# Soft combine: subtracting the maxima of the last logit tiles on VectorE instead of in TensorE's accumulation

## The reference

```python
def _L1_ffn_ref(x, phi_w, phi_b, expert_w, expert_b):      # x: tokens x 128
    logits = x @ phi_w.T + phi_b                 # tokens x 2048, seen as (n = 64 experts, p = 32 slots)
    D = softmax(logits over p)                   # dispatch weights
    C = softmax(logits over n)                   # combine weights
    X_tilde = layernorm(clip(D.T @ x)); X_tilde = tanh(X_tilde)
    Y_tilde = X_tilde[n] @ expert_w[n] + expert_b[n]       # 2048 slots x 128
    return C @ Y_tilde
```

## Time and profile before

| | |
|---|---|
| median of 3 executions | 2280.3 us (2280.26, 2280.30, 2286.44) |
| profiled execution | 2283.84 us, its span 2281.8 us |
| PE busy | 1911.1 us (84%) |
| DVE busy | 1573.7 us (69%) |
| ACT busy | 1187.5 us (52%) |
| POOL busy | 1204.3 us (53%) |
| logits, f32 products (L1889) | 512 records, 261.8 us |
| logits, bf16 products (L1890) | 256 records, 96.8 us |
| combine (L1916) | 512 records, 226.7 us |

### The profile page before, as it was taken

One profiled execution on the slowest core, in us unless ns is written; L12 is line 12 of the kernel. 1 busy time (PEld: TensorE's weight loads), 2 busy tenths in 40 slices (PEclk: granted clock), 3 DMA queues, 4 the chain that ended last, 5 costly groups with the idle time before them and its releaser, 6 DMA issues.

```text
span 2281.8 us, 24245 instructions
## 1 busy us (share of the span) xinstructions
PE 1911.1 (84%) x6152; PEld 923.1 (40%) x6152; DVE 1573.7 (69%) x2040; ACT 1187.5 (52%) x2832; POOL 1204.3 (53%) x779
## 2 busy tenths in 40 slices
PE   4099676888888725978999899997987999899998
PEld 3077522333333513764333344443333333344443
DVE  7033487999999831338999665764895999855544
ACT  2322286555555341217999643342446999753332
POOL 4645104999999574535999400000983999800000
PEclk9999896999999957989999999998988999999999
DMA  8122472444545122333000000001633000000000
GB/s 263 57 88 89 109 129 110 174 176 169 180 168 177 54 68 67 102 119 93 0 0 0 1 1 1 0 0 51 180 111 90 3 0 0 0 1 10 5 9 14
DMA packets 108478, 163.50 MB, mean 72 GB/s; under 512 B 11144, under 2 KB 74051, under 8 KB 108273
## 3 DMA queue, kind: packets, MB, share of 16 engines
q1 hardware_dynamic: 100210, 146.29, 21.4%
q0 software_dynamic: 8192, 16.30, 2.1%
HBM read 124.97 MB, written 38.14 MB: 71 GB/s over the span
## 4 chain that ended last, share of the span: by engine, by line
PE 49%; DVE 21%; issue 13%; POOL 11%; ACT 3%; DMA 2%; DVEq 0%; POOLq 0%; SPq 0%; ACTq 0%
PE ps L1916 10%; PE ps L1889 10%; PE ps L1645 5%; PE ps L1655 5%; PE ps L1845 4%; DVE arena L1396 3%; PE ps L1836 3%; DVE arena L1402 3%; DVE arena L1394 3%; POOL slot_inputs L504 3%; PE ps L1771 3%; PE ps L1890 2%; DVE arena L1341 2%; POOL arena L558 2%; POOL arena L594 1%
## 5 line engine op out<-in xcount | busy, mean ns | idle before, releaser
L1845 PE MATMUL ps<-arena 128*128 128x512 f32 x512 | 250.9, 613 | 14.3 <-POOL arena L558 14.2
L1889 PE MATMUL ps<-XT,c_phiT 128*128 (+1 forms) x512 | 261.8, 593 | 0.0
L1836 PE MATMUL ps<-c_phiT,arena 128*128 128x512 f32 x512 | 245.9, 604 | 9.7 <-DVE arena L1396 7.0
L566 POOL TENSOR_TENSOR arena<-arena 128x864 f32<-128x864 f32 x128 | 210.1, 1642 | 78.5 <-DVE arena L1394 75.8
L558 POOL TENSOR_TENSOR arena<-arena 128x1024 f32<-128x1024 f32 x128 | 244.6, 1912 | 0.0
L532 POOL TENSOR_TENSOR arena<-XT,arena 128x1024 f32<-128x1024 f32 x86 | 169.7, 1993 | 134.6 <-DMA arena<-input_gates 134.6
L1916 PE MATMUL ps<-arena 128*128 128x512 f32 x512 | 226.7, 601 | 11.1 <-DVE arena L1460 11.1
L594 POOL TENSOR_TENSOR arena<-arena 128x1024 f32<-128x1024 f32 x32 | 63.6, 2000 | 309.9 <-DMA arena<-value_rows 309.9
L1460 DVE TENSOR_TENSOR arena<-arena 128x4096 f32<-128x4096 f32 x32 | 140.2, 4422 | 121.0 <-ACT arena L899 121.0
L892 ACT ACTIVATE arena<-ps 128x512 f32<-128x512 f32 x256 | 152.0, 597 | 111.4 <-PE ps L1890 111.3
L514 POOL DMA_INDIRECT token_outputs<-arena x128 | 124.3, 971 | 148.3 <-DVE arena L1236 114.7
(11 more groups left out here) (229 smaller groups left out, 3597.3 us busy)
## 6 DMA issues: line engine op xcount, KB each, us to landing
arena<-input_gates SPq DMA_DIRECT2D x128, 512.0 KB, 3.8
arena<-value_rows SPq DMA_DIRECT2D x32, 512.0 KB, 4.8
arena<-slot_inputs SPq DMA_DIRECT2D x32, 258.0 KB, 2.8
arena<-in_L_ffn_w SPq DMA_DIRECT2D x32, 256.0 KB, 4.0
arena<-token_outputs SPq DMA_DIRECT2D x16, 512.0 KB, 7.4
slot_inputs<-arena SPq DMA_DIRECT2D x1, 4128.0 KB, 13.4
slot_inputs<-zero SPq DMA_DIRECT2D x1, 4128.0 KB, 33.3
token_outputs<-arena SPq DMA_DIRECT2D x1, 4096.0 KB, 17.5
```

Of the source, the lines that this page charges most:

```text
L566: pool.tensor_tensor(Ed[:, r, PSLOT * NA:].rearrange("p (n q) -> p n q", q=PSLOT), Lc[:, r, PSLOT * NA:].rearrange("p (n q) -> p n q", q=P ...
L1836: ins = pe.matmul(pbank(2 * h + c), xts[:, r // 2, :], phiT[:, at:at + CHUNK], start=True, stop=True)
L1845: ins = pe.matmul(pbank(4 + 2 * h + c), xns[:, r // 2, :], Dd[:, r, CHUNK * c:CHUNK * (c + 1)], start=start, stop=stop, skip_group_check=True)
L1889: pe.matmul(pbank(t % 4), phiT[:, P * t:P * (t + 1)], xt(b, c), start=True, stop=False)
```

## The change

In the six chunks of the loop, the last tiles of a chunk lose their bf16 product. `BY_PE = (11, 9)` is the number of tiles that keep it: in stage 0 tiles 11 to 15 (5 of them) go without, in stage 1 tiles 9 to 15 (7 of them). In place of these products:

- TensorE does the bf16 product once more, alone, into bank 4, ahead of tile 4. It waits for the logarithm of the chunk before (`lnz`), which was the last to read bank 4.
- ScalarE copies bank 4 into a new 128 x 512 tile `mS` in SBUF, ahead of the exponential of tile 6, after the wait for tile 6.
- VectorE adds `mS` to each of the last tiles, from PSUM into `Ec[c]` (`less_m`). In its order this stands at the start of a chunk, ahead of `ln_apply` and the tree.
- ScalarE's exponential of these tiles waits for the addition and runs in place on `Ec[c]`.

Some semaphores are merged: `Z` becomes `bank4`, `Rz` becomes `token_rows`, `g_diff` and `gates` in the experts become one. The experts' instructions stay as they were.

```diff
+BY_PE = (11, 9)
...
+        mS = cut([CHUNK])
...
                         if t == 0 and not first:
                             hold(act, sem("yT_ps"), v - 1)
-                        act.activation(Ec[c][:, t, :], pbank(t % 4), ACT.Exp)\
-                            .then_inc(sem("Ec"), 1)
+                        if not first and t == 6:
+                            hold(act, sem("bank4"), sums_count(s, v) - 1)
+                            act.activation(mS, pbank(4), ACT.Copy).then_inc(sem("token_rows"), 1)
+                        logit = pbank(t % 4)
+                        if not first and t >= BY_PE[s]:
+                            hold(act, sem("less_m"), less_m_count(s, v, t))
+                            logit = Ec[c][:, t, :]
+                        act.activation(Ec[c][:, t, :], logit, ACT.Exp).then_inc(sem("Ec"), 1)
...
+                def less_m(v, c):
+                    dve.wait_ge(sem("token_rows"), sums_count(s, v) - 1)
+                    dve.wait_ge(sem("yT_ps"), v - 1)
+                    for t in range(BY_PE[s], ST):
+                        dve.wait_ge(sem("LT"), ST * v + t + 1)
+                        dve.tensor_tensor(Ec[c][:, t, :], pbank(t % 4), mS, ALU.add).then_inc(sem("less_m"), 1)
...
                 with dve.Fori(1, CHUNKS // 2) as i:
+                    less_m(base + 2 * i, 0)
                     if s == 0:
                         ln_apply(4, 2 * i - 2, 0)
                     normalise(base + 2 * i, 0)
                     residual(base + 2 * i - 1, i - 1, 1)
+                    less_m(base + 2 * i + 1, 1)
...
-                        pe.matmul(pbank(t % 4), phiT[:, P * t:P * (t + 1)], xt(b, c), start=True, stop=False)
-                        pe.matmul(pbank(t % 4), row128[:, :],
-                                  mCT[:, ds(b * TIME + CHUNK * c, CHUNK)], start=False, stop=True).then_inc(sem("LT"), 1)
+                        m = mCT[:, ds(b * TIME + CHUNK * c, CHUNK)]
+                        if loop and t == 4:
+                            pe.wait_ge(sem("lnz"), v)
+                            pe.matmul(pbank(4), row128[:, :], m, start=True, stop=True).then_inc(sem("bank4"), 1)
+                        without_m = loop and t >= BY_PE[s]
+                        ins = pe.matmul(pbank(t % 4), phiT[:, P * t:P * (t + 1)], xt(b, c), start=True, stop=without_m)
+                        if not without_m:
+                            ins = pe.matmul(pbank(t % 4), row128[:, :], m, start=False, stop=True)
+                        ins.then_inc(sem("LT"), 1)
```

More of the change, by code:

```diff
@@ L296, in over, with sums_count, less_m_count @@
             return t.unsqueeze(2).to_broadcast([t.shape[0], t.shape[1], n])
+        def sums_count(s, v):
+            return v - CHUNKS * s + (2 * CHUNKS - 2) * s + 1 if isinstance(v, int) else 2 * (v - s)
+        def less_m_count(s, v, t):
+            return (ST - BY_PE[s]) * (v - CHUNKS * s - 2) + t - BY_PE[s] + 1 + s * (ST - BY_PE[0]) * (CHUNKS - 2)
         def below(i, n):
@@ L659, in experts @@
             def experts(m, k):
-                hold(act, sem("g_diff"), m + 1)
+                hold(act, sem("gates"), 2 * m + 1)
                 act.activation(g1[5], g1[4], ACT.Exp).then_inc(sem("g_exp"), 1)
@@ L665, in experts @@
                     chain(act.activation(A_neg[:, :, :], A_neg[:, :, :], ACT.Copy, scale=-1.0))
-                hold(act, sem("gates"), m + 1)
+                hold(act, sem("gates"), 2 * m + 2)
                 for q in range(K):
@@ L891, in exp_T @@
                             hold(act, sem("yT_ps"), v - 1)
-                        act.activation(Ec[c][:, t, :], pbank(t % 4), ACT.Exp)\
-                            .then_inc(sem("Ec"), 1)
+                        if not first and t == 6:
[6 more added lines that the diff above has]
+                        act.activation(Ec[c][:, t, :], logit, ACT.Exp).then_inc(sem("Ec"), 1)
                 def finish(v):
-                    hold(act, sem("Z"), v + 1)
+                    hold(act, sem("bank4"), sums_count(s, v))
                     act.activation(lnz, pbank(4), ACT.Ln).then_inc(sem("lnz"), 1)
                     hold(act, sem("lnz"), v + 1)
-                    act.activation(Rz, lnz, ACT.Exp, scale=-1.0).then_inc(sem("Rz"), 1)
+                    act.activation(Rz, lnz, ACT.Exp, scale=-1.0).then_inc(sem("token_rows"), 1)
                 def copy_y(v):
@@ L1201, in experts @@
                 ok = g64[1].rearrange("p (a b) -> p a b", b=TILES)
-                dve.tensor_tensor(d21, g1[1], g1[0], ALU.subtract).then_inc(sem("g_diff"), 1)
+                dve.tensor_tensor(d21, g1[1], g1[0], ALU.subtract).then_inc(sem("gates"), 1)
                 chain(dve.tensor_scalar(ok, place, CAP + 0.5, None, ALU.is_lt))
@@ L1456, in normalise @@
                         dve.tensor_tensor(dst, lo, hi, ALU.add).then_inc(sem("tree"), 1)
-                    dve.wait_ge(sem("Rz"), v + 1)
+                    dve.wait_ge(sem("token_rows"), sums_count(s, v))
                     for g in range(2):
@@ L1881, in soft, with logits_T @@
                 base = CHUNKS * s
-                def logits_T(v, b, c, early, beside=None):
+                def logits_T(v, b, c, early, beside=None, loop=False):
                     for t in range(ST):
@@ L1907, in total @@
                     pe.wait_ge(sem("tree"), 5 * (v + 1))
-                    pe.matmul(pbank(4), same_p[:, :], t1, start=True, stop=True).then_inc(sem("Z"), 1)
+                    pe.matmul(pbank(4), same_p[:, :], t1, start=True, stop=True).then_inc(sem("bank4"), 1)
                 def combine(v, c, early):
@@ L1938, in soft @@
                         v = base + 2 * i + c
-                        logits_T(v, i, c, False)
+                        logits_T(v, i, c, False, loop=True)
                         combine(v - 1, 1 - c, False)
```

## The result

| | before | changed |
|---|---|---|
| median, 6 executions each | 2285.14 us (2280.26 to 2287.33) | 2270.24 us (2269.16 to 2272.29) |
| profiled execution, its span | 2283.84, 2281.8 us | 2269.76, 2267.8 us |
| PE, DVE, ACT busy | 1911.1, 1573.7, 1187.5 us | 1901.0, 1618.9, 1192.8 us |

The ratio of the times is 0.994, 95% interval 0.993 to 0.9951: the changed kernel is 0.6% faster. The medians of six lie 14.9 us apart. Three further executions of the kernel before, taken beside the changed one, were at 2284.83 to 2287.33 us, above two of the three that the prediction started from.

What follows compares the result with a forecast made beforehand. TensorE alone was taken to bound the loops: net 60 products x 0.215 = 12.9 us, less 0.2 of stalls, so 2280.3 - 12.7 = 2267.6 us. The range was 2264.5 to 2272.5 us, the forecast's own 2266.5 to 2270.

Steps and rivals of the forecast that it cites:

- What bounds the kernel: Combine loops of both stages: TensorE alone sets the time, so a removed bf16 product is worth its full 0.215 us.
- The sum: Both stages' loops: 12.9 us from a net 60 products, less 0.2 us of small stalls, gives 12.7 us.
- the narrower range: Whole kernel's time with full gain but for small stalls: 2266.5 to 2270 us, chance 0.74.
- (a): Stage 0, tile 15: additions begin late, at 13.55 us into a chunk, leaving tile 15 a slack of 0.1 us.
- The exponential from SBUF: ScalarE, last tiles: reading SBUF instead of PSUM takes 0.63 instead of 0.60 us; the skill page estimates 0.04 more.
- The addition: VectorE, last tiles: each of 72 additions of 128 x 512 from PSUM takes 0.68 us.
- The slower case: VectorE's additions in both stages become the bound; above 1.46 us each the kernel is slower than before; chance 0.03.
- my formula: Waits by addition length L: stage 0's tile 15 L - 0.80 us, stage 1's 3L - 2.9 above L = 0.97.
- (b): Stage 1, tile 13: additions start when tile 9 is ready at 11.0 us, slack 0.5 us, and none falls behind.
- (c): End of a chunk: the tree ends later but before `total` needs it, slack 3.2 us in stage 0, 3.8 in stage 1.
- Rival 3: Outside the loops, between the stages: TensorE's clock drops move, changing the time by a few us; upward gain's chance 0.07.
- A reading: Profile slices of the combine: VectorE (DVE) was read at 5 to 9 in slices 23 to 27.

## Why the prediction was right

- **What bounds the kernel.** Right. Every product taken from TensorE's stream in the loops came back whole, at 0.215 us, in every trace.
- **The sum.** 12.7 us were forecast for the two loops, 12.5 measured: 4.80 of stage 0's 5.17 and 7.71 of stage 1's 7.74. The time itself fits less well, and that 2270.24 us lies in the range is in part luck. The predicted median, 2267.6 us, started from 2280.3, but the median of six executions of the kernel before is 2285.14, 4.8 higher; and the difference is 14.9 us and not 12.7, since stretches outside the loops gave 2.4 us. The two errors go against each other. The measured time is just above the narrower range of 2266.5 to 2270. The ratio, 0.994, agrees with the forecast's own 0.9944.
- **(a), the edge at tile 15.** The place was right, and two terms were mis-sized against each other. The exponential of tile 11 ended 15.09 us after the chunk's start in an odd chunk (15.15 forecast), because VectorE's end and ScalarE's start are 0.09 us apart and not 0.28, while the first addition started at 13.68 and not 13.55. There is no stall in odd chunks, though the weight load of tile 15 is 0.1 us late, so the slack is used up. In even ones VectorE's loop starts a round in just this gap, the addition starts at 14.08 and the exponential ends at 15.50: 0.18 us of stall, in chunks 4 and 6. I had 0.2 us for the sum of these, and 0.36 came.
- **The exponential from SBUF.** 627 against 597 ns, 0.03 us, as L899 had shown. The Trainium skill's 0.04 ("VectorE: DVE Perf Modes", section "The TRN2 errata — SBUF-src ops pay a fixed extra latency per instruction") has the sign and nearly the size.
- **The addition.** 690 ns against 0.68. The slower case would have needed 1.46 us by my formula. With each addition done twice, 1.20 us from pair to pair, the loops lost 5.0 of their 12.5 us, where the prediction had put 6.6 for an addition of 1.20. So the formula overstates the losses, by the 0.10 us now known between the engines among others; the 1.46 itself was not tried.
- **(b) and (c).** Right to 0.4 us: in stage 1 the additions wait for their tiles. The tree of stage 0 ends 26.95 us into the chunk (27.3 forecast) and the total comes at 30.49 (30.5). In stage 1 it is 25.5 (25.8) and 29.63 (29.6).
- **Rival 3**, a shift outside, was real, and it came on top of the forecast instead of in its place: -3.1 us between the stages, +0.6 ahead of stage 0 and +1.0 at the end, 1.5 us in all. The prediction had named a move of more than 2 us between the stages as a sign against its forecast; it came, and the loops still did what was forecast. Of the 3.1, 2.6 are of the kind that the rival names, a shift that moves TensorE's clock drops; 1.4 are not, but come from VectorE's loop in stage 1's dispatch, and 0.9 are lost again around it, most of them by the clock. At the end the granted clock over the last combine is 0.86 instead of 0.91, and the changed kernel's second trace has the same (28.11 us against 27.27 in the kernel before's). Between the stages and at the end the length repeats from trace to trace of a kernel. Ahead of stage 0 that isn't shown: there the 0.6 us are small against the 5 us by which kernels on one chip differ.
- **A reading.** VectorE's slices in stage 0's combine stand at 5 to 7, not 5 to 9. Nothing rests on it.

## What to carry to other kernels

Where one engine's stream has no gap, a piece of work moved off it is worth its distance in that stream; what it costs on the other engines is decided by when they are free, when their input is ready and when the result is needed back, counted from the start of a round, not by their busy share. When the helper is late, look first at what stands ahead of it in its own order: here 2.7 us of statistics moved behind three additions turned a loop that lost 6 us against the kernel before into one that gained 7.8. A few tenths of slack belong where the helper's own loop starts a round. And gains of one or two us are judged by stretches of the trace that hold the change, since stretches without it moved by as much here.

## What the runs showed of the hardware

- VectorE, at the start of a round of its loop: 0.55 us from the last operation to the first, where the same two operations within a round are 0.14 apart. In another loop, the dispatch's, a round's start leaves it idle for 0.12 us in stage 0 of every kernel, and in stage 1 for 0.25 us in the five traces without the additions and 0.12 in the eight with them.
- From the end of a VectorE operation to the start of the ScalarE activation that waits for it directly: 0.09 to 0.10 us. Where more of ScalarE's instructions stood between wait and activation, 0.28.
- Two f32 additions of 128 x 512 with one operand in PSUM, back to back on VectorE, start 0.60 us apart though each record is 0.69 long (2119.78, 2120.39).
- TensorE's clock behind an idle time of 1.66 us stayed at full for the chunk, behind 2.07 us the chunk's mean was 0.95, and a stall of 2.1 us cost 4.0 in all.
- The pattern of TensorE's clock drops in the attention was the same in two traces of each of two kernels, taken on different chips, and another one when a stage ahead of it was 1.3 us shorter: 2.0 us of 156.7 in the attention and 0.6 ahead of it, as much as 12 of the products moved here.
